# First attention: probabilities transposed unscaled, output scaled by transposed reciprocals, output product a turn later

## The reference

```python
q, k, v = (proj(wq), proj(wk), proj(wv))
q = _apply_rope(q, sin, cos)
k = _apply_rope(k, sin, cos)
scores = jnp.einsum('bnth,bnsh->bnts', q, k) * (1.0 / math.sqrt(h))
scores = jnp.where(causal, scores, -jnp.inf)
attn = jax.nn.softmax(scores, axis=-1)
out = jnp.einsum('bnts,bnsh->bnth', attn, v)
out = out.transpose(0, 2, 1, 3).reshape(B, T, C)
return jnp.einsum('btc,dc->btd', out, wo)
```

## Time and profile before

| What | Value |
|---|---|
| median of 3 runs | 1597.06 us (1591.18 to 1598.67) |
| the profiled execution | 1588.73 us, of which span 1586.9 us |
| PE, DVE, ACT, POOL busy over the span | 90%, 71%, 46%, 27% |
| first attention, start of its first maxima to its last output product's end | 51.7 to 355 us |
| reciprocals and scalings in it | 64 and 256 instructions on DVE |
| TensorE clock granted, mean | 0.976 of full speed |

### The profile page before, as it was taken

One profiled execution on the slowest core, in us unless ns is written; L12 is line 12 of the kernel. 1 busy time (PEld: TensorE's weight loads), 2 busy tenths in 40 slices (PEclk: granted clock), 3 DMA queues, 4 the chain that ended last, 5 costly groups with the idle time before them and its releaser, 6 DMA issues.

```text
span 1586.9 us, 26588 instructions
## 1 busy us (share of the span) xinstructions
PE 1430.3 (90%) x9332; PEld 1215.0 (77%) x9332; DVE 1120.2 (71%) x2171; ACT 735.7 (46%) x1996; POOL 432.0 (27%) x328
## 2 busy tenths in 40 slices
PE   4888888869999797899999999999999999958998
PEld 3776767547777585788888988889888988846887
DVE  6686868678999853546776778767687767863554
ACT  3675757532222221425555555555555555532332
POOL 5100000003223370433343241434243342315000
PEclk9999999999999999699999999999999999988999
DMA  6000010113322000210202010020202120010000
GB/s 198 28 1 28 1 57 10 40 41 102 118 79 73 7 14 2 74 34 28 67 28 67 26 33 33 26 66 26 66 26 66 26 66 14 13 47 20 15 13 26
DMA packets 39681, 67.80 MB, mean 43 GB/s; under 512 B 4940, under 2 KB 13799, under 8 KB 39618
## 3 DMA queue, kind: packets, MB, share of 16 engines
q1 hardware_dynamic: 37522, 65.69, 13.2%
q10 hardware_dynamic: 2096, 1.30, 0.3%
HBM read 60.65 MB, written 2.13 MB: 40 GB/s over the span
## 4 chain that ended last, share of the span: by engine, by line
PE 59%; DVE 21%; issue 13%; POOL 3%; ACT 3%; DMA 1%; SPq 0%; POOLq 0%; DVEq 0%; ACTq 0%
PE PS L325 14%; PE PS L327 14%; PE PS L326 14%; DVE E_p L1253 3%; DVE A_mx L1024 2%; DVE E_nb L1244 2%; DVE E_mx L1240 2%; PE PS L1793 2%; DVE A_pT L1011 2%; DVE E_T L1262 1%; PE PS L1776 1%; PE PS L1459 1%; PE PS L1491 1%; POOL E_sw L526 1%; PE PS L1480 1%
## 5 line engine op out<-in xcount | busy, mean ns | idle before, releaser
L325 PE MATMUL PS<-XNH,E_WL 128*128 128x256 f32 x768 | 218.1, 284 | 6.7 <-POOL E_WL L440 5.9
L326 PE MATMUL PS<-XNL,E_WH 128*128 128x256 f32 x768 | 214.4, 279 | 0.0
L327 PE MATMUL PS<-XNH,E_WH 128*128 128x256 f32 x768 | 214.2, 279 | 0.0
L526 POOL TENSOR_TENSOR E_sw<-E_sw,rope2s 128x1024 f32<-128x1024 f32 x64 | 103.3, 1615 | 309.9 <-ACT E_sw L578 309.9
L1240 DVE TENSOR_REDUCE E_mx<-PS 128x4 f32<-128x512 f32 x64 | 60.8, 951 | 139.2 <-PE PS L1779 139.2
L325 PEld LDWEIGHTS PS<-XNH,E_WL 128*128 128x128 f32 x768 | 144.7, 188 | 11.1 <-POOL E_WL L440 8.9
L326 PEld LDWEIGHTS PS<-XNL,E_WH 128*128 128x128 f32 x768 | 144.5, 188 | 1.0
L327 PEld LDWEIGHTS PS<-XNH,E_WH 128*128 128x128 f32 x768 | 144.4, 188 | 0.0
L791 ACT ACTIVATE E_p<-PS,E_nb 128x128 f32<-128x128 f32 (+1 forms) x256 | 103.8, 431 | 85.1 <-DVE E_nb L1244 85.1
L578 ACT ACTIVATE E_sw<-PS 64x256 f32<-64x256 f32 (+1 forms) x128 | 89.5, 699 | 103.8 <-PE PS L327 102.3
L440 POOL TENSOR_TENSOR E_WL<-raw,E_WH 128x512 fp32r<-128x512 f32 x80 | 102.7, 1319 | 124.6 <-ACT E_WH L578 124.6
(11 more groups left out here) (266 smaller groups left out, 4260.3 us busy)
## 6 DMA issues: line engine op xcount, KB each, us to landing
raw<-in_w SPq DMA_DIRECT2D x104, 256.0 KB, 2.9
words<-in_words SPq DMA_DIRECT2D x11, 768.0 KB, 4.3
wo<-in_wo SPq DMA_DIRECT2D x32, 256.0 KB, 3.9
zb<-z_scratch SPq DMA_DIRECT2D x11, 384.0 KB, 5.1
scb<-in_scales SPq DMA_DIRECT2D x11, 384.0 KB, 5.6
X<-in_x SPq DMA_DIRECT2D x8, 256.0 KB, 5.7
SGH<-XNH SPq DMA_DIRECT2D x8, 256.0 KB, 2.7
SGL<-XNL SPq DMA_DIRECT2D x8, 256.0 KB, 2.9
```

The source lines that it names most:

```text
L325: nc.tensor.matmul(o, sl, mh, start=first, stop=False)
L326: nc.tensor.matmul(o, sh, ml, start=False, stop=False)
L327: return nc.tensor.matmul(o, sh, mh, start=False, stop=last)
L526: nc.gpsimd.tensor_tensor(E_sw[:, heads, :], E_sw[:, heads, :], rope2s[:, :].unsqueeze(1).broadcast_to([P, heads.stop - heads.start, SEQ]) ...
```

## The change

- DVE no longer scales the probabilities. They are transposed and multiplied by the values unscaled. DVE takes one reciprocal of all eight sums per turn (L1065 of the changed kernel).
- POOL's `spread` copies each reciprocal over the 16 channels of its head (two multiplications by one, 64 elements each, into `A_rx`, which lies in `raw`), behind the sines of the same turn. Two turns make one 128-column block per token tile.
- PE transposes the two blocks after `weighted_values` of an odd group, that is in even turns, into the free half of bank 4. ACT's `take_reciprocals` copies them to `A_R` (also in `raw`), behind `stack_heads`. DVE's `weigh` multiplies bank 4 by `A_R` into `OT0`; it takes the place of the copy L1046 and stands behind `rotate`.
- `output` and `add_branch` move from turns 0 and 1 to turns 1 and 2 of the next batch, and both token tiles use bank 2, so the second waits for the first one's addition. DVE's `add_branch` stands behind `weigh`.
- In batch 3 POOL's `scale_tile` moves into turns 3 to 5.

```diff
--- before.py
+++ after.py
@@ -122,6 +122,8 @@
                 A_nb = sb(st, "A_nb", [P, 8])
                 A_sum = sb(st, "A_sum", [P, 8])
                 A_rec = sb(st, "A_rec", [P, 8])
+                A_rx = raw[:, 3, 0:2 * P].rearrange("p (b r) -> p b r", b=2)
+                A_R = raw[:, 4, 0:SEQ]
 
             with phase() as mid:
 
...
@@ -457,11 +459,34 @@
                 nc.gpsimd.tensor_tensor(A_sw[:, :, :], A_sw[:, :, :], rope0s[:, tl, :].unsqueeze(1).broadcast_to([P, H0 // 2, D0]), ALU.mult)\
                   .then_inc(a["t2"], 1)
 
+            def spread(b, g):
+
+                t = b * G0 + g
+                pool.wait_ge(a["rec"], t + 1)
+                if g % 2 == 0:
+                    after(pool, a["rt"], b * KT + g // 2)
+                one = mask01[:, P - 1:P].unsqueeze(2).unsqueeze(3).broadcast_to([P, 2, 2, D0])
+                for tb in range(2):
+                    o = A_rx[:, tb, 64 * (g % 2):64 * (g % 2) + 64].rearrange("p (n e d) -> p n e d", n=2, e=2)
+                    i = A_rec[:, 4 * tb:4 * tb + 4].rearrange("p (e n) -> p n e", e=2).unsqueeze(3).broadcast_to([P, 2, 2, D0])
+                    last = nc.gpsimd.tensor_tensor(o, i, one, ALU.mult)
+                last.then_inc(a["rx"], 1)
+
             def attend(b):
                 for g in range(G0):
                     unit = prepared(b, g)
                     if unit:
                         sines(unit[0], unit[3])
+                    spread(b, g)
+                    if isinstance(b, int) and b == NB - 1 and 3 <= g < 6:
+                        scale_tile(0, 0, (g - 3,))
+
+            def scale_tile(n, p, weights=(0, 1, 2)):
+                for c in weights:
+                    pool.wait_ge(f["t"], n * 3 + (c + 1))
+                    if not isinstance(n, int) or n >= 1:
+                        pool.wait_ge(f["lo"], n * 3 + (c - 2))
+                    nc.gpsimd.tensor_tensor(F_w[:, c, :], F_t[:, c, :], scb[p][:, c, :], ALU.mult).then_inc(f["w"], 1)
 
             for g in FIRST:
                 unit = prepared(-1, g)
...
@@ -661,6 +676,12 @@
                 act.wait_ge(a["pt"], t * 2 - 1)
                 after(act, a["pv"], t - 1)
                 copy(A_pT[:, 0:4, :], PS[:, 5, :].rearrange("p (h t) -> p h t", h=4), a["pe"])
+
+            def take_reciprocals(pairs):
+
+                act.wait_ge(a["rt"], pairs)
+                after(act, a["ot"], pairs - 1)
+                copy(A_R[:, :], PS[:, 4, SEQ:2 * SEQ], a["rc"])
 
             def attend(b):
                 for g in range(G0):
@@ -685,6 +706,8 @@
                         take_values(unit)
                     if unit:
                         stack_heads(unit)
+                    if g % 2 == 0 and turn_before(b, g):
+                        take_reciprocals(b * KT + g // 2)
                     if isinstance(b, int) and b == NB - 1 and 4 <= g < 7:
                         ffn_heads(0, 0, (g - 4,))
 
...
@@ -1013,7 +1037,12 @@
             def add_branch(b, tl):
                 dve.wait_ge(a["wo_ps"], b * 2 + (tl + 1))
                 xt = X[:, bass.ds(b * 2 + tl, 1), :].rearrange("p a c -> p (a c)")
-                V.tensor_tensor(xt, xt, PS[:, 3 - tl, :], ALU.add).then_inc(a["x"], 1)
+                V.tensor_tensor(xt, xt, PS[:, 2, :], ALU.add).then_inc(a["x"], 1)
+
+            def weigh(pairs, k):
+
+                dve.wait_ge(a["rc"], pairs)
+                V.tensor_tensor(OT0[:, k, :], PS[:, 4, 0:SEQ], A_R[:, :], ALU.mult).then_inc(a["ot"], 1)
 
             def attend(b):
                 later = not isinstance(b, int) or b >= 1
@@ -1031,24 +1060,18 @@
                         stack_rests(earlier)
                     if turn_before(b, g):
                         take_probabilities(t)
-                    for tb in range(2):
-                        dve.wait_ge(a["exp"], t * 2 + (tb + 1))
-                        V.reciprocal(A_rec[:, 4 * tb:4 * tb + 4], A_sum[:, 4 * tb:4 * tb + 4]).then_inc(a["rec"], 1)
-                        dve.wait_ge(a["rec"], t * 2 + (tb + 1))
-                        for n in range(4):
-                            blocks = slice(n, n + 1) if tb == 0 else slice(4 + 2 * n, 6 + 2 * n)
-                            ins = V.tensor_scalar(A_ps[g % 2][:, blocks, :], A_ps[g % 2][:, blocks, :], A_rec[:, 4 * tb + n:4 * tb + n + 1], None, ALU.mult)
-                        ins.then_inc(a["pn"], 1)
-                    if g % 2 == 0 and (g or later):
-                        dve.wait_ge(a["pv"], t)
-                        if g == 2:
-                            after(dve, a["wo_ps"], b * 2)
-                        V.tensor_copy(OT0[:, (g // 2 - 1) % KT, :], PS[:, 4, 0:SEQ]).then_inc(a["ot"], 1)
+                    dve.wait_ge(a["exp"], t * 2 + 2)
+                    after(dve, a["rx"], t)
+                    V.reciprocal(A_rec[:, :], A_sum[:, :]).then_inc(a["rec"], 1)
                     if unit:
                         cosines(unit)
                         rotate(unit)
-                    if g < 2 and later:
-                        add_branch(b - 1, g)
+                    if g % 2 == 0 and (g or later):
+                        if g == 2:
+                            after(dve, a["wo_ps"], b * 2)
+                        weigh(b * KT + g // 2, (g // 2 - 1) % KT)
+                    if 1 <= g < 3 and later:
+                        add_branch(b - 1, g - 1)
                     if isinstance(b, int) and b == NB - 1:
                         if g == 3:
                             dve.wait_ge(a["vps"], 4 * NB)
@@ -1072,8 +1095,7 @@
                 attend(b)
             attend(NB - 1)
             take_probabilities(NB * G0)
-            dve.wait_ge(a["pv"], NB * G0)
-            V.tensor_copy(OT0[:, KT - 1, :], PS[:, 4, 0:SEQ]).then_inc(a["ot"], 1)
+            weigh(NB * KT, KT - 1)
             for tl in range(2):
                 add_branch(NB - 1, tl)
             finish(dve, 2)
@@ -1483,19 +1505,26 @@
                                 last = mm(PS[rows32, 4, P:SEQ], stationary, A_pT[:, 8 + h, :], start=False, stop=(e == 1),
                                           skip_group_check=True, tile_position=(0, 32 * c))
                 last.then_inc(a["pv"], 1)
+                if g % 2:
+                    pe.wait_ge(a["rx"], t)
+                    for tb in range(2):
+                        last = nc.tensor.transpose(PS[:, 4, SEQ + tb * P:SEQ + (tb + 1) * P], A_rx[:, tb, :], ident[:, :])
+                    last.then_inc(a["rt"], 1)
 
             def output(b, tl):
                 if tl == 0:
                     pe.wait_ge(a["ot"], b * 4 + 4)
+                else:
+                    pe.wait_ge(a["x"], b * 2 + 1)
                 for k in range(KT):
-                    last = mm(PS[:, 3 - tl, :], OT0[:, k, tl * P:(tl + 1) * P], wo0[:, k, :], start=(k == 0), stop=(k == KT - 1))
+                    last = mm(PS[:, 2, :], OT0[:, k, tl * P:(tl + 1) * P], wo0[:, k, :], start=(k == 0), stop=(k == KT - 1))
                 last.then_inc(a["wo_ps"], 1)
 
             def probabilities(t, g, unit, stacks):
 
 
                 for tb in range(2):
-                    pe.wait_ge(a["pn"], t * 2 + (tb - 1))
+                    pe.wait_ge(a["exp"], t * 2 + (tb - 1))
                     if tb == 0 and unit:
                         pe.wait_ge(a["t1"], unit[0] + 1)
                     if tb == 1 and stacks:
@@ -1529,8 +1558,8 @@
                     if g % 4 == 0:
                         pe.wait_ge(a["ev"], b * G0 + (g + 4))
                     pe.wait_ge(a["vcp"], b * 4 + (2 + sum(g > v for v in (1, 2, 5, 6) if prepared(b, v))))
-                    if later and g in (1, 2):
-                        pe.wait_ge(a["x"], b * 2 + (g - 2))
+                    if later and g in (2, 3):
+                        pe.wait_ge(a["x"], b * 2 + (g - 3))
                     scores(g)
                     if turn_before(b, g):
                         probabilities(t, g - 1, earlier, prepared(b, g, 2))
@@ -1543,8 +1572,8 @@
                     if turn_before(b, g):
                         weighted_values(t, (g - 1) % G0, b * KT + (g - 1) // 2)
                     pe.wait_ge(a["exp"], t * 2 + 2)
-                    if g < 2 and later:
-                        output(b - 1, g)
+                    if 1 <= g < 3 and later:
+                        output(b - 1, g - 1)
                     if unit and g % 4 in (1, 2):
                         values(unit)
 
```

More of the change, by code:

```diff
@@ L276, in sems @@
             return {n: sem(f"{prefix}_{n}") for n in names.split()}
-        a = sems("a", "stage0 stage1 init proj sw t1 t2 q hi lo tp ev vps vcp sc mx neg exp rec pn pt pe pd pv ot wo_ps x")
+        a = sems("a", "stage0 stage1 init proj sw t1 t2 q hi lo tp ev vps vcp sc mx neg exp rec rx rt rc pt pe pd pv ot wo_ps x")
         def prepared(b, g, ago=0):
@@ L472, in _ @@
             attend(NB - 1)
[L475 to L482, removed]
             finish(pool, 2)
@@ L706, in _ @@
             take_probabilities(NB * G0)
```

(1 more changed line is left out.)

## The result

The changed kernel took 1616.59 us (median of 4 runs, 1613.19 to 1618.24), the kernel before 1594.55 in the same series: ratio 1.0134 [1.0100, 1.0169], slower by 1.3%, some 21 us. The forecast was +16.6. The profiled execution took 1613.19 us, 24.5 more than the one of before.

The account below looks back on a forecast made before the run. A serial loop of hand-overs (maxima, stack transposes, swap, sines, A_q) was taken as the bound, neither PE nor DVE full. Terms 4.5 - 10.5 + 17.1 + 1.8 + 3.9 - 0.2 = +16.6 us gave 1613.7 us, range 1600 to 1624.

Parts of the forecast that it names:

- the main mechanism: DVE in even turns: weigh waits for ACT's reciprocals' copy, next maxima queue behind; +1.5 us in plain turns, g=2 +5.7.
- the scalings at nothing: DVE, each turn: about 2 us of scalings and reciprocals removed, costed at nothing; last four turns -3 to +2 us.
- the output product alone: Output product a turn later: g=0 loses 3.7 us of product, 0.5 of wait, 0.9 of addition; g=2 gains the product.
- the even turns with values: g=2 of batch 0, g=6 of batches 0 to 2: two transposes and weigh's late end, +0.45 us each, +1.8.
- I expect A_q, two SBUF inputs, to wait for the first spread only: 0.3 us: DVE's A_q held by POOL's first spread in 13 plain turns with projections, 0.3 us each: +3.9 us.
- the spread never holds A_q: Rival: POOL's spread does not delay DVE's A_q; +12.7 us, 1609.8 us; chance 0.20.
- the chance of the lower clock: Rival: PE, idle longer, drops from 2.4 to 1.2 GHz; stack transposes doubled in 13 turns, +14 us, 1628; chance 0.05.
- The end: After the last turn: path loses 1.4 us, gains 0.8, and the second product waits 0.9 for the first's addition: +0.3.

Follow-up runs that it names:

- the first experiment: Kernel before with DVE's eight scalings of the probabilities left out, output not divided by the sums: 1591.33 against 1594.31 us, ratio 0.9986.

## Why the prediction was right or wrong

**Right, the main mechanism.** Weigh waits for ACT's copy in every even turn, and maxima stand behind it: g=4 is 8.97 to 8.99 us (9.0 forecast), g=0 is 9.03 and 8.95 where no gap comes in (9.0), g=2 is 15.16 and 15.23 (15.2) where the clock is whole. The wait is 1.06 us and ends with ACT's copy into raw. With the copy moved ahead, the 1.5 us of g=4 shrink to 0.3 and the 2.0 of g=2 go; with the addition moved ahead, the 2.0 go alone. The reciprocals' copy took 0.36 to 0.39 us (0.38 taken).

**Right, the scalings at nothing** in turns with a rotation, by the first experiment; the 2 to 3 us that it gained lie in the last turns, for which the forecast allowed -3 to +2. **Right, the output product alone**: -4.5 us in its turns with no weigh in them.

**Too large, the even turns with values**: +0.28 us for 0.45. That is the two transposes' 0.27; the 0.2 for a weigh that ends after the scores did not appear.

**Wrong: "I expect A_q, two SBUF inputs, to wait for the first spread only: 0.3 us", +3.9 us.** The runs show nothing: g=3 and g=7 are 7.48 to 7.53 us, A_q 0.44 after 0.43. Two things went wrong. The operations were mis-sized, 0.28 us each for 0.45. And the prediction read the earlier trace rows as a loser that waits to the end of the other's operation: E_T takes 1.21 us where no POOL operation runs beside it (at 718.18 us), so of its 1.96 us 0.75 were the wait, 0.13 less than the 0.88 that POOL's operation still had. A_nb likewise waited 0.45 of 0.60 us. A_q began 0.13 us into a spread of 0.28 (half of the 0.56 at 217.63); with some 0.13 off the remaining 0.15, next to nothing is left, as measured. The longer operation fits too: 0.61 - 0.14 - 0.14 = 0.33 us, and A_q took 0.76 for 0.42 at 140.40:

```profile
140.26 0.61 POOL L469 TENSOR_TENSOR raw<-mask 128x256 f32<-128x256 f32 x1
140.40 0.76 DVE L1025 TENSOR_TENSOR A_q<-A_T,A_sw 128x256 f32<-128x256 f32 x1 [0.43 <-POOL A_sw L459]
```

With the operations at 0.45 the same reckoning would have given 0.2 us, an estimate. The rival "the spread never holds A_q" is what came, and with it 1609.8 us would have been the forecast.

**Wrong, the chance of the lower clock.** It had 0.05, and a price of 14 us, stack transposes doubled in all 13 turns. It came in part, in some turns that change in part from run to run, and not where the price had it: in g=1 of the last batch the stack transposes took their 1.09 us, and the weighted values behind them 1.92 for 1.06. In the profiled execution g=5 of the first two batches, g=1 and g=2 of the last and g=3 of the third are longer by 1.6, 1.6, 1.6, 0.7 and 0.5 us than the waits explain, 6.0 together.

**Missed: the gap on ACT.** No row of before hinted at it. g=0 of the third batch is 4.1 us longer than the forecast 9.0, 2.3 by the gap and 1.8 by the clock behind it.

The account of the +22.8 us in the turns: g=4 three times +1.5, g=0 three times -3.5, g=2 three times +5.7, four even turns with values +0.28, together 12.2; the gap 2.3; the clock 7.8; the last turns and roundings 0.5. Without its +3.9 the forecast would have said +12.7, close to the 12.2 of the waits; the lower clock and the gap added 10 that it did not have. Its +16.6 came near the +21 measured because these two errors offset each other in part, which is luck. Luck as well is part of how near the 1613.7 us are to the 1616.59 measured: they were reckoned from a median of 1597.06 us, and the series that holds both kernels has 1594.55. The end was taken at +0.3 us and measured +0.6.

## What to carry to other kernels

An engine that is busy for 6.6 of 7.5 us of a turn can still have work that lies outside the loop of hand-overs: leaving the scalings out bought 2 to 3 us, in the last turns, and one added wait in that engine's in-order list cost some 21. Where a dependent operation is added, put its input's producer ahead of whatever that producer's engine queues for others, and the operation ahead of the head of the loop: one copy moved ahead of two to four others was worth 21 us here. Look also at what waits behind it one step further, the addition and PE's scores.

Count second costs of a wait too. PE standing longer can lose its clock behind the wait, and in the profiled execution the clock was a third of the loss (7.8 of 22.8 us, of which 1.8 behind ACT's gap).

## What the runs showed of the hardware

**A loop's branch back can cost ACT 2 to 3 us, and did so with the longer lists.** The gap is in all seven traces of kernels that have ACT's reciprocals' copy, 2.8 to 3.1 us, and in the one with three more copies, 2.0; it is in none of the five with ACT's list in the turns as before and not in the one with one more copy. The loop's body has 169 instructions on ACT before, 173 with one more copy, 177 after and 181 with three more, readouts of the sums and separate waits on semaphores not counted; with those waits it has 203, 207, 214 and 215. In the stretch around the branch of the changed kernel (204 to 211 us) the instruction queue moves data, where the kernel before has none at the same place:

```profile
DMA packets 3, 0.02 MB, mean 4 GB/s; under 512 B 0, under 2 KB 0, under 8 KB 0
...
q14 instruction: 3, 0.02, 1.4%
```

Over the whole program that queue moved 32 packets in the kernels with the gap and 26 or 27 in those without. From the page, the changed kernel:

```profile
q14 instruction: 32, 0.26, 0.1%
```

and the kernel before:

```profile
q14 instruction: 27, 0.22, 0.0%
```

The Trainium skill (Runtime: NRT & Kernel Launch, Instruction fetch mechanics) says that a branch back to a place no longer held in the engine's instruction memory must fetch it before work goes on. These rows agree. Where the limit lies they show only as between 173 and 177 instructions for this loop at this place. The list ahead of the loop grew in the same runs, so whether the loop's length or its place decides, no run tells apart.

**A short GpSimd operation did not hold up a VectorE operation that it overlapped; a longer one did.** 64 elements: A_q 441 ns; 256 elements: 750 ns, in both cases begun about 0.13 us after POOL. The Trainium skill (SBUF — State Buffer, SBUF: two separate sides) has whichever starts first hold the pair for its whole instruction. By the recorded times the loser waited 0.13 to 0.15 us less than that in all four cases: E_T 0.75 of 0.88 us, A_nb 0.45 of 0.60, A_q 0.34 of 0.47 behind the long operation and 0.02 of 0.15 behind the short one. So both agree if the pair comes free some 0.13 us ahead of the recorded end, which is inferred from these rows; what happens inside that time no run shows.

**The granted clock fell in some turns and not in others of the same kind.** g=5 of the first batch was at 0.85 in one execution of the changed kernel and took its full-clock time of 9.49 us in another; the mean of both was 0.969. Between g=2 of the first batch and g=2 of the last, all five traces in which maxima wait behind ACT's late copy have three to seven turns with a mean clock below 0.97. The nine others have none, but for the turn with ACT's gap in three of them. In the last turns, where PE has less to do, the clock also fell in kernels without that wait: g=3 of the last batch is 8.8 to 8.9 us for 7.27 in the run with only the output product a turn later and in the one with one more copy. Ten transposes of work that nobody needs, in turns where PE would have waited anyway, made the kernel faster.
